# Reordered queues in a fused adaLN block: the first gelu, k's remainder, the third parts and the stack transfers each move to another place in their engine's order

## What is computed

```python
h = _layernorm(x) * (1 + ca) + sa
x = x + ga * attention(h)          # q = h @ w_dq.T @ w_uq.T; k, v from h @ w_dkv.T @ w_ukv.T; 16 heads of 16, causal softmax
h = _layernorm(x) * (1 + cb) + sb
x = x + gb * ffn(h)                # two experts (gelu, relu), 256 -> 512 -> 256, the better of two gate scores picks per token
```

## Time and profile before

| | |
|---|---|
| median of three timed runs | 622.9 us (622.04 to 628.52) |
| the profiled execution | 623.6 us, span of its instructions 621.8 us |
| busy in the span | TensorE 518.4 us (83%), VectorE 461.5 (74%), ScalarE 390.9 (63%), GpSimd 305.9 (49%) |
| mean granted TensorE clock | 0.943 of full speed |
| DMA | 43.74 MB, mean 70 GB/s; the queue of SyncE 37.3% of 16 engines' span |

### The profile page before, as it was taken

One profiled execution on the slowest core, in us unless ns is written; L12 is line 12 of the kernel. 1 busy time (PEld: TensorE's weight loads), 2 busy tenths in 40 slices (PEclk: granted clock), 3 DMA queues, 4 the chain that ended last, 5 costly groups with the idle time before them and its releaser, 6 DMA issues.

```text
span 621.8 us, 14267 instructions
## 1 busy us (share of the span) xinstructions
PE 518.4 (83%) x4912; PEld 456.4 (73%) x4912; DVE 461.5 (74%) x884; ACT 390.9 (63%) x585; POOL 305.9 (49%) x300
## 2 busy tenths in 40 slices
PE   5634667899898979989898989799898998989974
PEld 4423455688787969787877878697778897878773
DVE  3438172689898987888887889877788888785373
ACT  2424454767777767676776767676667776676521
POOL 6235232355565554556454555555464564552352
PEclk9957595999999998999998999999899999999998
DMA  8644363433425170706253352608062524201100
GB/s 267 154 54 73 47 82 60 75 65 58 100 46 110 30 127 1 145 9 101 53 77 77 51 103 37 116 0 150 4 94 63 76 62 77 63 1 37 35 17 18
DMA packets 43802, 43.74 MB, mean 70 GB/s; under 512 B 5344, under 2 KB 40800, under 8 KB 43760
## 3 DMA queue, kind: packets, MB, share of 16 engines
q1 hardware_dynamic: 43760, 43.19, 37.3%
HBM read 13.39 MB, written 4.23 MB: 28 GB/s over the span
## 4 chain that ended last, share of the span: by engine, by line
PE 62%; DMA 10%; issue 9%; SPq 8%; ACT 6%; DVE 4%; POOL 0%; ACTq 0%; POOLq 0%; DVEq 0%
DMA ks<-parts_k 7%; PE ps_s L382 7%; PE ps_t L402 6%; PE ps_t L419 5%; SPq L282 4%; PE ps_c L333 4%; PE ps_t L406 4%; PE ps_c L335 4%; PE ps_c L334 4%; PE ps_o L333 3%; PE ps_o L334 3%; PE ps_a L333 3%; PE ps_o L335 3%; PE ps_a L334 3%; PE ps_a L335 3%
## 5 line engine op out<-in xcount | busy, mean ns | idle before, releaser
L1248 POOL TENSOR_SCALAR_AFFINE_SELECT score_rows<-score_rows 128x512 f32<-128x512 f32 (+1 forms) x96 | 83.3, 869 | 135.6 <-ACT score_rows L792 135.6
L792 ACT ACTIVATE score_rows<-ps_s 128x1024 f32<-128x1024 f32 x96 | 98.6, 1027 | 75.5 <-PE ps_s L382 69.1
L944 DVE TENSOR_REDUCE mx<-score_rows 128x4 f32<-128x1024 f32 (+1 forms) x96 | 115.4, 1212 | 18.4 <-POOL score_rows L1248 18.4
L816 ACT ACTIVATE p<-ps_t 128x1024 f32<-128x1024 f32 x96 | 98.6, 1027 | 15.7 <-PE ps_t L406 15.0
L382 PE MATMUL ps_s<-ks,qs 96*128 96x256 bf16 (+1 forms) x512 | 63.1, 260 | 43.7 <-DMA ks<-parts_k 29.4
L382 PEld LDWEIGHTS ps_s<-ks,qs 96*128 96x128 bf16 x512 | 38.3, 103 | 55.9 <-issue 44.2
L402 PE MATMUL ps_t<-qs,ks 99*128 99x256 bf16 (+1 forms) x512 | 61.8, 255 | 10.2 <-DMA qs<-mx_rows 9.7
L1182 POOL TENSOR_TENSOR xs<-z,xs 128x512 f32<-128x512 f32 (+1 forms) x16 | 25.0, 1562 | 66.0 <-DVE z L1033 66.0
L1090 DVE CAST hid_hi<-hid 128x512 fp32r<-128x512 f32 x64 | 34.9, 545 | 24.4 <-ACT hid L782 23.3
L402 PEld LDWEIGHTS ps_t<-qs,ks 99*128 99x128 bf16 x512 | 39.5, 101 | 15.9 <-issue 6.3
L1236 POOL TENSOR_TENSOR hid_lo<-hid,hid_hi 128x512 fp32r<-128x512 f32 x32 | 42.9, 1354 | 7.9 <-DVE hid_hi L1090 7.9
(11 more groups left out here) (165 smaller groups left out, 1666.4 us busy)
## 6 DMA issues: line engine op xcount, KB each, us to landing
qs<-parts_q SPq DMA_DIRECT2D x96, 128.0 KB, 4.3
ks<-parts_k SPq DMA_DIRECT2D x96, 128.0 KB, 5.0
xs<-x SPq DMA_DIRECT2D x16, 256.0 KB, 4.8
gates<-gates_scratch SPq DMA_DIRECT2D x16, 256.0 KB, 4.1
out<-xs SPq DMA_DIRECT2D x16, 256.0 KB, 4.2
p<-wmod SPq DMA_DIRECT2D x1, 1024.0 KB, 6.2
p<-waT SPq DMA_DIRECT2D x1, 1024.0 KB, 8.4
p<-wmod SPq DMA_DIRECT2D x1, 512.0 KB, 5.4
```

The costliest lines, as they stand in the source:

```text
L792: act.activation(score_rows[c % 2][:], ps_s[:], ACT.Copy).then_inc(scores_out, 1)
L816: act.activation((p0, p1)[tile][:, h0:h0 + n, :], ps_t[:].rearrange("p (h s) -> p h s", h=n), ACT.Exp, scale=SCALE).then_inc(exp_done, 1)
L944: dve.tensor_reduce(dst, score_rows[c % 2][:].rearrange("p (h k) -> p h k", h=n), AX_X, ALU.max).then_inc(max_done, 1)
L1248: pool.affine_select(out=diag, in_=diag, compare_op=ALU.is_ge, fill=NEG, base=0, pattern=[[0, n], [-1, P]], channel_multiplier=1).then_inc ...
```

## The change

ScalarE: `gelu(b, 0)` goes from the head of a step to the tail of the step before, ahead of the two value copies. VectorE: `k_rest` and `k_second` go between the last two row maxima. GpSimd: the third parts go ahead of the gating, the wait for the split stands behind both of them, and `hidden_low(b, 0)` ahead of `add_ffn`. SyncE: all 12 stacks are issued ahead of the maxima, the gates, the store and the next x; the gates wait for `scaled` in place of `out_ready`.

```diff
@@ SyncE, load_gates @@
-                wait(sp, out_ready, b.n - 1)
+                wait(sp, scaled, b.n - 1)
@@ SyncE, step @@
                 stack_q(at(0), 1)
                 stack_k(at(0), 0)
                 stack_q(at(0), 2)
+                stack_k(at(0), 1)
+                stack_k(at(0), 2)
                 load_maxima(at(1))
                 load_gates(at(2))
-                stack_k(at(0), 1)
                 store(at(4))
                 prefetch_x(at(-2))
-                stack_k(at(0), 2)
@@ ScalarE, step @@
             def step(at):
-                gelu(at(4), 0)
                 maxima_rows(at(2))
                 gelu(at(4), 1)
@@
                 scores_copy(at(1), 5)
                 k_first(at(0))
+                gelu(at(3), 0)
                 values_copy(at(2), 0)
                 values_copy(at(2), 1)
@@ VectorE, step @@
                 row_max(at(2), 4)
+                k_rest(at(1))
+                k_second(at(1))
                 row_max(at(2), 5)
                 split_maxima(at(2))
-                k_rest(at(1))
                 hidden_high(at(4), 0)
-                k_second(at(1))
@@ GpSimd, step @@
                 hide_scores(at(1), 5)
+                q_third(at(0))
+                k_third(at(0))
+                leave_to_split(at(1))
                 gate_ffn(at(4))
+                hidden_low(at(3), 0)
                 add_ffn(at(4))
-                q_third(at(0))
-                leave_to_split(at(1))
-                k_third(at(0))
-                hidden_low(at(3), 0)
```

## The result

The changed kernel takes 638.7 us (635.8 to 640.4, four runs) against 623.7 for the kernel before in the same comparison: ratio 1.022, interval [1.015, 1.030]. It is slower, by 1.5 to 3%. The forecast was 633.7 us, +1.7%, with a range of 606 to 646. The profiled execution took 640.24 us, 16.6 more than the profiled one of before.

A forecast was written before the change was run, and what follows sets the result against it. TensorE, busy 83% of the span, was taken as the bound, with two holes per steady step. Terms -0.8 + 14.3 - 2.7 = +10.8 us on the profiled 623.6 gave 634.4, or 633.7 us against the median; range 606 to 646.

The forecast's parts named there:

- Part 1, the gelu: ScalarE's earlier first gelu removes TensorE's 1.37 us hole ahead of turn_maxima, with no more table loads.
- Part 2, VectorE and GpSimd: k's remainder between the row maxima: split's cast and subtraction give back 1.9 us for 1.1; cost +1.1 to -0.8, hidden.
- Part 3, the stacks: Twelve stacks back to back on SyncE: k complete 14.3 us into the step, hole ahead of s_chunk 0 gone.
- Part 4, the maxima: Maxima queue behind twelve stacks, landing 14.5 us into the step; new TensorE hole of 2.3 to 3.4 us at st_chunk 0.
- 11.7 plus three stacks: Bound for the maxima's landing: 11.7 us with nine stacks ahead, plus three at 1.0 each, 14.7 us into the step.
- The late VectorE: VectorE runs later against TensorE: a 1.07 us wait ahead of expand_k, falling inside the new hole at no further cost.
- The clock: TensorE's granted clock falls behind the new hole in nine of twelve steps, at 1.59 us each: +14.3 us.
- The sum for twelve steps: Steady steps of 33.54 us against 33.61, -0.8 us over twelve, plus +14.3 us for clock falls.
- The end of the run: The two last boundaries with turn_values, with no stacks behind, gain the gelu's 1.35 us each: -2.7 us.
- the maxima pass the stacks: Rival: maxima not held up in the transfers, both old holes and the clock falls go; 595 us, chance 0.2.
- the clock stays up: Rival: TensorE's clock does not fall through the new hole, so the 14.3 us are not lost; 619.4 us, chance 0.22.
- Everything late adds up: Rival: clock falls in all twelve steps (+4.8 us) and each landing 0.5 us later (+6); 644.5 us, chance 0.13.

The follow-up runs named there:

- the fast variant: The changed kernel with load_maxima moved ahead of stack_k 1 and 2, so nine stacks precede the maxima instead of twelve: 589.1 us, ratio to before 0.947.
- The filled hole: The changed kernel with 20 useless 128x256 products on TensorE ahead of its wait for the maxima: 629.1 us, ratio to before 1.015.

## Why the prediction was right, and where it was off

*Part 1, the gelu.* Right. The hole is gone, no table load was added, and the second value copy starts as soon behind its products as before. Alone it gives 2.4%.

*Part 2, VectorE and GpSimd.* Right that it changes nothing in the sum, as far as the fast variant shows it; from the changed kernel itself these orders were not taken out. The split's cast takes the 181 ns that I took (before: the earlier trace rows):

```profile
L957 DVE CAST mx_parts<-mx_rest x16: 181/181/182, 59.9 to 572.9; 128x32 bf16<-128x32 f32 x16
```

`k_second` takes 502 ns in the median and 1.3 us at worst where it took 0.42: the loss beside `q_third` that was allowed for, behind the same cover. The two orders do this by themselves: done alone in the kernel before, they bring all 16 casts of the split to 181 or 182 ns; taken out of the fast variant, nine of the 16 take 1.08 to 1.15 us again. The rule that the prediction took from the Trainium skill, GPSIMD Engine Reference, Specifications, named the cast as one of the operations to gain, and the trace agrees. What I had not seen is how dear these orders are without the rest of the change.

*Part 3, the stacks.* Right: k is no longer waited for.

*Part 4, the maxima.* The mechanism is as forecast: one hole in each steady step, with `mx_rows` as its releaser. Its size was off. I took A + 14.5; the mean of the twelve starts of `st_chunk` 0 is A + 15.1. The step that failed is "I take A + 14.5, the nearest row being the first step". The first step had twelve stacks but no maxima behind them, so 24 KB at 130 GB/s, 0.2 us, was set for these. Measured in the twelve steps, k's last stack lands at A + 14.6 in the mean (14.3 in the sum), the maxima 0.45 us behind it, at A + 15.0, and TensorE starts 0.07 us later: each term is a little too small. The other bound, "11.7 plus three stacks", 14.7, was too low as well, since with nine stacks ahead the maxima land at A + 12.1 in the later steady steps and not at 11.7. What makes this difference between early and later steps stays open. Filling TensorE's hole did not change it.

*The late VectorE.* Right: a wait for `ckv` of 0.45 to 1.1 us shows ahead of `expand_k` in all steady steps but the first, and it falls inside the new hole, which is 2.5 to 3.6 us.

*The clock.* Nine falls at 1.59 us were forecast, 14.3 us. There were six: four cost some 1.5 us each, as taken, and two 2.7, where the clock stayed low for longer. From the time between `st_chunk` 0 and `s_chunk` 0 (3.73 us without a fall) they come to 11.5 us. The filled hole gives 11.6 by another way.

The sum for twelve steps, forecast and found: landing -0.8 and +7.3 more; falls 14.3 and 11.5; from `st_chunk` 0 to `s_chunk` 0 3.73 in place of 3.88, -1.8; from there to the next A 15.26 in place of 15.16, +1.2. Found in all -0.8 + 7.3 + 11.5 - 1.8 + 1.2 = 17.4, and the trace has 12 x (35.05 - 33.61) = 17.3. The end of the run gave back 0.7 us and not 2.7: the last step with stacks, which the sum left out, lost 0.7 (`s_chunk` 0 at A + 18.75 against 18.03), and all behind it gained 1.4. That the total came within 5 us is in part luck: the late landing, the way to the next A and the end of the run came out 10.5 us above the forecast together, and fewer falls and the shorter way to `s_chunk` 0 took 4.6 off again.

*The rivals.* That the maxima pass the stacks is refuted, even on a queue of their own. That the clock stays up happened in half of the steps, and with the hole filled in all. "Everything late adds up" was half right: the landing came 0.6 us later, but the falls were fewer.

## What to carry to other kernels

When transfers are reordered, count the bytes that go ahead of each of them: a small urgent transfer behind large ones waits for their whole backlog, about a microsecond per 128 KB here, and another queue doesn't help. The gain was in the same edits: the small one before the last large ones, and the bulk that nobody waits for at the very end. And try the parts of a change singly as well as together: of the orders of four engines here, ScalarE's gains 2.4% alone, SyncE's costs 4% alone, and those of VectorE and GpSimd together cost 7.5% alone and nothing in the fast variant.

## What was not expected of the hardware

- A transfer of 24 KB on a queue of its own, issued at A + 8.3 into a backlog of another queue, had its first packet at A + 14.2 and released TensorE at A + 15.75, behind all that had been issued before it.
- Of holes of the same length, the granted clock stayed up behind one of 3.34 us and fell behind one of 3.36. In the changed kernel it fell behind six of twelve, though all of them (2.5 to 3.6 us) were longer than the 2.00 us that had sufficed once in the kernel before.
